# One-bank score units in an attention core, and re-ordered start and end of a state-space stage

## Time and profile before

| | us |
|---|---|
| median of 3 runs | 2258.87 |
| lowest and highest | 2258.38, 2261.21 |
| the profiled execution, its own time | 2256.16 |
| its span (first to last instruction) | 2253.9 |
| mean granted clock of TensorE | 0.987 of full |

### The profile page before, as it was taken

The page is one execution under the profiler, slowest core; times in us unless marked ns, Lnnn a source line. Parts: engine busy times, 40 slices in busy tenths (PEclk is TensorE's granted clock), DMA queues, the critical chain, the costliest instruction groups (busy, mean ns, idle before and its releaser), DMA issues. The chain is left out here.

```text
span 2253.9 us, 34737 instructions
## 1 busy us (share of the span) xinstructions
PE 2149.1 (95%) x12556; PEld 1748.4 (78%) x12556; DVE 1676.1 (74%) x2693; ACT 1434.7 (64%) x3086; POOL 1038.2 (46%) x759
## 2 busy tenths in 40 slices
PE   7889989999899999999999999999999999997999
PEld 7856677887688878878887887887887888785887
DVE  7667755133688898889889889889988988986221
ACT  4377734333877677677777767766877677673332
POOL 5466535443146344444435533634445443545442
PEclk9999999999999999999999999999999999998999
DMA  3000012331333233223322323223322322231332
GB/s 131 1 1 1 1 43 61 94 94 57 141 113 108 94 117 122 85 86 140 122 85 85 141 94 113 97 94 129 107 100 85 141 108 100 85 113 40 92 95 83
DMA packets 64151, 202.50 MB, mean 90 GB/s; under 512 B 7024, under 2 KB 8048, under 8 KB 55664
## 3 DMA queue, kind: packets, MB, share of 16 engines
q1 hardware_dynamic: 63984, 200.31, 25.9%
HBM read 197.39 MB, written 2.88 MB: 89 GB/s over the span
## 5 line engine op out<-in xcount | busy, mean ns | idle before, releaser
L529 POOL TENSOR_TENSOR wAl<-rawA,wAh 128x512 fp32r<-128x512 f32 x233 | 325.8, 1411 | 406.1 <-ACT wAh L670 405.4
L1599 PE MATMUL ps<-xTh,wAh 128*128 128x512 f32 x1512 | 427.3, 404 | 7.9 <-DVE oacc L1437 3.0
L1599 PE MATMUL ps<-xTl,wAh 128*128 128x512 f32 x1512 | 415.0, 396 | 0.0
L1599 PE MATMUL ps<-xTh,wAl 128*128 128x512 f32 x1512 | 413.9, 395 | 0.0
L1332 DVE SCALAR_TENSOR_TENSOR work<-ps,chp,work 128x510 f32<-128x510 f32 (+2 forms) x465 | 343.5, 744 | 51.6 <-ACT work L829 41.6
L1599 PEld LDWEIGHTS ps<-xTl,wAh 128*128 128x128 f32 x1512 | 284.9, 188 | 69.7
L1599 PEld LDWEIGHTS ps<-xTh,wAh 128*128 128x128 f32 x1512 | 276.6, 189 | 78.4 <-issue 17.5
L1599 PEld LDWEIGHTS ps<-xTh,wAl 128*128 128x128 f32 x1512 | 283.6, 188 | 69.3
L535 POOL TENSOR_TENSOR wBl<-rawB,wBh 128x512 fp32r<-128x512 f32 x108 | 142.2, 1330 | 386.1 <-ACT wBh L674 386.1
L866 ACT ACTIVATE eb<-eb,gc 128x128 f32<-128x128 f32 x1008 | 307.7, 391 | 18.0 <-DMA eb<-scr_decays 18.0
L579 POOL TENSOR_TENSOR sqt<-gt 128x512 f32<-128x512 f32 x112 | 154.4, 1379 | 120.6 <-DVE gt L1391 112.1
(11 more groups left out here) (202 smaller groups left out, 3958.5 us busy)
## 6 DMA issues: line engine op xcount, KB each, us to landing
eb<-scr_decays SPq DMA_DIRECT2D x63, 1536.0 KB, 6.4
rawA<-ma_in SPq DMA_DIRECT2D x144, 256.0 KB, 3.6
rawA<-fa_in SPq DMA_DIRECT2D x88, 256.0 KB, 2.6
rawB<-mb_in SPq DMA_DIRECT2D x64, 256.0 KB, 2.8
rawB<-fb_in SPq DMA_DIRECT2D x44, 256.0 KB, 2.6
x<-x_in SPq DMA_DIRECT2D x8, 256.0 KB, 6.2
x_out<-x SPq DMA_DIRECT2D x8, 256.0 KB, 2.7
wqraw<-wqkv_in SPq DMA_DIRECT2D x1, 1536.0 KB, 10.9
```

Of the source, the lines that this page charges most:

```text
L529: nc.gpsimd.tensor_tensor(wAl[:, slot, :], rawA[:, slot, :], wAh[:, slot, :].bitcast(F32), ALU.subtract).then_inc(A_lo, 1)
L1599: return nc.tensor.matmul(o, l, r, start=start, stop=end, **kw)
```

## The change

All parts are order and tiling; the result is the same function.

- Attention. A unit is at most one bank: a narrow unit as before, a wide one in two halves h of two heads by 256 keys each, so there are 24 of them for a batch. They rotate over banks 2 to 5, so TensorE waits for the exponentials of the fourth unit back. The mask matmul of a half has 256 columns. The maximum is negated in the reduction itself, the factor 1/4 is put into the copy of the keys, and the small second instruction is gone. Transposes to banks 6 and 7 are signalled separately. On TensorE the order inside a wide unit is scores h=0, (value products), transposes of bank 6, scores h=1, transposes of bank 7. The last tile's head transposes move behind the scores of unit 3; the fill of the second key block on GpSimd moves ahead of the last tile's split.
- Start of the state-space stage. The chunk-end sums are copied out first (`end_sums`) and TensorE waits for that copy alone. The rows for step 1 are loaded straight after the first rows, and their chunk starts come as plain sums, exponentiated in place by `second_exp`.
- End. The swiglu's first four weight tiles are loaded, and split on ScalarE and GpSimd, one step earlier; the last step's decays, `scale_x` and transposes move ahead; `y_products` come before the `last_out` of the step before; ScalarE squares the last step's y into xdt, and `last_squares` sums sq and xdt with twice the matmuls.

The phrase "rebuilt expert stages" in the name of the change has nothing in the diff: the experts' code is the same on both sides. The core of the diff:

```diff
...
+    UNITS = 24
+    def unit(n, h=0):
+        b, s = n // 16, n % 16
+        return UNITS * b + (s if s < 8 else 8 + 2 * (s - 8) + h)
+    def unit_heads(n, h):
+        return range(4) if n % 16 < 8 else range(2 * h, 2 * h + 2)
+    def second_halves(n):
+        return 8 * (n // 16) + max(0, n % 16 - 7)
...
+            else:
+                for u in range(4):
+                    load_A(a0 + u, fa_in[u // 2, u % 2])
             for h in range(2):
                 for f in range(NF):
                     for u in range(2):
-                        load_A(a0 + (h * NF + f) * 2 + u, fa_in[f, u])
+                        n = (h * NF + f) * 2 + u
+                        if first or n >= 4:
+                            load_A(a0 + n, fa_in[f, u])
...
         first_rows(1)
+        sp.dma_start(eb[:, 1, :, 0:NT, :], scr[2:4, 0:NT, :].partition_broadcast(P)).then_inc(m_rows[1], 16)
+        for h in range(2):
+            sp.dma_start(eb[:, 1, h, NT:NT + B, :],
+                         scr[2 + h, 1:NT:2, :].partition_broadcast(P)).then_inc(m_second, 16)
         mamba_B(2, 0)
...
         sp.wait_ge(m_scr, 48)
-        mamba_rows(1, 0)
...
+            if t == NT - 1:
+                pool.wait_ge(a_proj, NT)
+                nc.gpsimd.memset(kBD[1][:, :, :, :, :].bitcast(F32), 0.0).then_inc(pads, 1)
+            if AHEAD + 2 <= t + 3 < NT:
+                layer_rstd(1, t + 3)
             pool.wait_ge(a_qh, t + 1)
             nc.gpsimd.tensor_tensor(qk[:, t % 2, 0:NH, HD:2 * HD].bitcast(F32R), qs[:, t % 2, :, :],
                                     qk[:, t % 2, 0:NH, 0:HD], ALU.subtract).then_inc(a_ql, 1)
...
+            if 3 <= t < 7:
                 pool.wait_ge(a_ql, t + 1)
-                key_lo(0, t - 4)
-                pool.wait_ge(a_kl, t - 3)
-        pool.wait_ge(a_proj, NT)
-        nc.gpsimd.memset(kBD[1][:, :, :, :, :].bitcast(F32), 0.0).then_inc(pads, 1)
+                key_lo(0, t - 3)
+                pool.wait_ge(a_kl, t - 2)
...
                 lo_A(A0G + i, g, NA_G)
+            if last and v == TPG - 2:
+                for u in range(4):
+                    lo_A(A0F + u)
...
         def finish():
-            for u in range(4):
-                lo_A(A0F + u)
-            lo_B(B0F)
-            square(TPG - 1, NG - 1, 0)
             last_rstd(0)
-            square(TPG - 1, NG - 1, 1)
             for t in range(AHEAD):
                 layer_rstd(5, t)
             last_rstd(1)
...
+        def exps(n, h):
+            m = unit(n, h)
+            heads = unit_heads(n, h)
+            wide = S if n % 16 >= 8 else P
+            act.wait_ge(a_nm, m + 1)
+            for i, j in enumerate(heads):
+                last = nc.scalar.activation(
+                    probs(n)[:, 0:wide // P, j, :],
+                    ps[:, 2 + m % 4, i * wide:(i + 1) * wide].rearrange("p (c k) -> p c k", k=P), ACT.Exp,
+                    bias=nm[:, m % 4, i:i + 1], accum_out=sm[:, n % RS, j:j + 1])
+            last.then_inc(a_exp, 1)
...
-                nk = 1 + s // 8
-                bank = 2 + 2 * (n % 2)
-                act.wait_ge(a_nm, n + 1)
+                if n == 2:
+                    act.wait_ge(a_qkt, NT - 1)
+                elif n == 3:
+                    queries(NT - 1)
                 if n >= PS_SLOTS:
                     act.wait_ge(a_tr, n - PS_SLOTS + 1)
+                    act.wait_ge(a_tr2, second_halves(n - PS_SLOTS))
                 if n >= RS:
                     act.wait_ge(a_rc, n - RS + 1)
-                for j in range(4):
-                    nc.scalar.activation(probs(n)[:, 0:nk, j, :],
-                                         ps[:, bank:bank + nk, j * P:(j + 1) * P], ACT.Exp,
-                                         bias=nm[:, n % 2, j:j + 1], scale=HD ** -0.5,
-                                         accum_out=sm[:, n % RS, j:j + 1]).then_inc(a_exp, 1)
+                exps(n, 0)
+                if s >= 8:
+                    exps(n, 1)
...
+            ending = last and v == TPG - 2
+            if ending:
+                hi_A(A0F)
+                hi_A(A0F + 1)
...
+            if ending:
+                hi_A(A0F + 2)
+                hi_A(A0F + 3)
...
-            decay_exp(*vn, 0)
-            decay_exp(*vn, 1)
+            if first and v == 0:
+                second_exp()
+            if not ending:
+                decay_exp(*vn, 0)
+                decay_exp(*vn, 1)
...
         def finish():
-            for u in range(4):
-                hi_A(A0F + u)
+            for p in range(2):
+                y_hi(NG - 1, TPG - 1, p)
+                nc.scalar.activation(xdt[:, 4 * p:4 * p + 4, :].rearrange("p t q -> p (t q)"),
+                                     gt[:, (TPG - 1) % 2, 512 * p:512 * p + 512], ACT.Square).then_inc(m_lsq, 1)
...
+        def end_sums(p):
             act.wait_ge(m_end, p + 1)
             nc.scalar.activation(wdt[:, 2 * p:2 * p + 2, :],
-                                 ps[:, YBANK[p], 0:2 * P].rearrange("p (b h) -> p b h", b=2), ACT.Exp).then_inc(m_u, 1)
+                                 ps[:, YBANK[p], 0:2 * P].rearrange("p (b h) -> p b h", b=2),
+                                 ACT.Copy).then_inc(m_ends, 1)
+        def end_decays():
+            act.wait_ge(m_ends, 2)
+            nc.scalar.activation(wdt[:, :, :], wdt[:, :, :], ACT.Exp).then_inc(m_u, 1)
+        def second_exp():
+            act.wait_ge(m_second, 32)
+            e = eb[:, 1, :, NT:NT + B, :].rearrange("p h t q -> p h (t q)")
+            nc.scalar.activation(e, e, ACT.Exp)
...
-        conv_silu(0, 4)
         conv_silu(0, 1)
         conv_silu(0, 3)
         gate_silu(0, 6)
+        end_sums(0)
+        end_sums(1)
+        conv_silu(0, 4)
+        conv_silu(0, 5)
         token_sums(1)
+        gate_silu(0, 7)
         spans(0, 0, 0)
-        conv_silu(0, 5)
-        gate_silu(0, 7)
-        hi_A(A0G + 5)
-        end_decay(0)
-        end_decay(1)
+        end_decays()
         first_exp(0)
         spans(0, 0, 1)
         first_exp(1)
+        hi_A(A0G + 5)
...
+            def negated_max(n, h):
+                m = unit(n, h)
+                heads = len(unit_heads(n, h))
+                dve.wait_ge(a_s, m + 1)
+                nc.vector.tensor_reduce(nm[:, m % 4, 0:heads], ps[:, 2 + m % 4, :].rearrange("p (j k) -> p j k", j=heads),
+                                        op=ALU.max, axis=AX.X, negate=True).then_inc(a_nm, 1)
...
-                    nk = 1 + n % 16 // 8
-                    bank = 2 + 2 * (n % 2)
-                    dve.wait_ge(a_s, n + 1)
-                    link(nc.vector.tensor_reduce(
-                        mx[:, n % 2, :], ps[:, bank:bank + nk, :].rearrange("p c (j k) -> p j c k", j=4),
-                        op=ALU.max, axis=AX.XY))
-                    if n >= 2:
-                        dve.wait_ge(a_exp, 4 * (n - 1))
-                    nc.vector.tensor_scalar(nm[:, n % 2, :], mx[:, n % 2, :], -HD ** -0.5, None,
-                                            ALU.mult).then_inc(a_nm, 1)
...
+                    negated_max(n, 0)
...
+                if n < N and n % 16 >= 8:
+                    negated_max(n, 1)
+                if 0 <= n - 1 < N:
+                    n1 = n - 1
+                    dve.wait_ge(a_exp, unit(n1, 1 if n1 % 16 >= 8 else 0) + 1)
...
+                if n == 3:
+                    keys(NT - 1)
...
+            elif k == 1:
+                dve.wait_ge(m_second, 32)
+                dve.wait_ge(m_exp, 3)
...
+            ending = last and v == TPG - 2
+            if ending:
+                decay_off(v + 1, g, 0)
+                decay_off(v + 1, g, 1)
...
+            if ending:
+                decay(v + 1, g, 0)
+                decay(v + 1, g, 1)
+                scale_x(v + 1, g, 0)
+                scale_x(v + 1, g, 1)
...
+            def scores(n, h):
+                b, s = n // 16, n % 16
+                qc, tt, r = s // 8, s // 4 % 2, s % 4
+                m = unit(n, h)
+                if m >= 4:
+                    pe.wait_ge(a_exp, m - 3)
+                t = 2 * b + qc
+                q = (xTh, xTl)[tt][:, r, t * P:(t + 1) * P]
+                to = ps[:, 2 + m % 4, :]
+                if qc == 0:
+                    mm(to, identb[:, :], negb[:, :, :].rearrange("p j k -> p (j k)"), True, False)
+                    mm(to, q, kBD[b % 2][:, 0, tt, :, 0:P], False, False)
+                    last = mm(to, q, kBD[b % 2][:, 1, tt, :, 0:P], False, True)
+                else:
+                    hi, lo = (kBD[b % 2][:, z, tt, 2 * h:2 * h + 2, :].rearrange("p j k -> p (j k)") for z in range(2))
+                    mm(to, q, hi, True, False)
+                    mm(to.rearrange("p (j k) -> p j k", j=2)[:, :, P:S], identb[:, :], negb[:, 0:2, :], False, False)
+                    last = mm(to, q, lo, False, True)
+                last.then_inc(a_s, 1)
...
-            pe.wait_ge(a_qt, 2 * NT)
-            pe.wait_ge(a_kt, NT)
-            pe.wait_ge(a_v, NT)
```

(51 more changed lines are left out.)

186 lines of the change are left out of this document (82 added, 104 removed).

## The result

The changed kernel takes 2221.5 us (median of four runs, 2220.6 to 2223.9) against 2259.6 for the kernel before on the same chip: ratio 0.9834, 95% interval 0.9822 to 0.9845, so 38 us less. The forecast was 2221.0, with a range from 2207 to 2238. The profiled execution of the changed kernel is the slowest of its four: own time 2223.9, span 2222.1, against 2256.2 and 2253.9 before.

What follows compares the result with a forecast made beforehand. TensorE is fullest, but in attention the chain around four engines sets the pace. Terms -14 - 6.5 - 2 - 6.5 - 9 = -38 take the profiled 2256.16 to 2218.2; the median, 2.7 above, gives 2221 us, range 2207 to 2238.

Steps and rivals of the forecast that it cites:

- Attention, steady part: Attention batches: four rotating banks loosen the coupling of engines, a batch falls from 43.9 to 40 us, -14 in all.
- the sum over quarters: Attention batch: largest engine load over each four units, work sliding only within them; 9.3, 9.2, 9.4, 11.6, sum 39.5 us.
- Rival 1: Attention units stay in step, so only start and tail gain, and perhaps 1 a batch; total -27.5, 2231; chance 0.17.
- rival 2: Attention: TensorE becomes the bound, a batch takes 36 to 37.5; total -49, 2210; chance 0.12.
- Rival 4: Attention: second-half scores come late behind transposes of unit n - 4; slower, 2273 at 1.2 a unit; chance 0.04.
- Attention, start and tail: Attention's ends: first scores fill TensorE's wait for the last tile's split, -6.5; tail transposes come closer together, -2.
- Start of the state-space stage: First state-space steps: rows for step 1 issued early, so ScalarE runs on without waiting for them; -6.5.
- A wait of 7.0 goes: State-space start: ScalarE's stand of 7.01 us until the rows for step 1 land disappears through their early issue.
- Rival 3: State-space start: early rows collide with the first rows on the DMA engines, start gains nothing; 2227; chance 0.06.
- End: Last state-space step: TensorE's waits for squares and decays, 8.52 us together, go; -9 (-6 to -11).
- The 7.58: State-space end: TensorE's wait for squares behind GpSimd's tile splits, removed as splits and squares both leave that place.
- the 0.94: State-space end: TensorE's wait for the last step's decays, 0.94 us, removed by moving them ahead of skip and gate.

Runs made afterwards that it cites:

- tile_wait: Changed kernel, but scores wait again for every exponential of the tile before last, with banks, halves and signals as changed: 2232.5 us (0.9878).
- heads_first: Changed kernel, but the last tile's head transposes stand before the first attention scores again: 2229.3 us (0.9864).
- start alone: Kernel before with only the rebuilt start of the state-space stage: 2254.3 us (0.9979).
- end alone: Kernel before with only the rebuilt end of the state-space stage: 2251.1 us (0.9965).

## Why the prediction was right

**Attention, steady part.** Forecast 40 a batch, measured 40.78; -14, measured -12.6. The term that was off is the sum over quarters: it gave 9.3, 9.2, 9.4, 11.6; the quarters measured from maximum to maximum (184.07, 193.11, 204.31, 212.68, 224.85) are 9.0, 11.2, 8.4, 12.2. Units 4 to 7 take 2.0 more than forecast, and this quarter gained nothing: before it was 11.1 (209.65 to 220.74). The matmuls that open the scores of unit 4 and of unit 8 say where the 2.0 is:

```profile
192.23 0.38 PE L1678 MATMUL ps<-negb,identb 128*128 128x512 bf16 x1
...
202.60 0.48 PE L1678 MATMUL ps<-kBD,xTh 128*128 128x512 f32 x1
```

In these 10.4 us TensorE does what the forecast counted for the quarter, 9.2 from start to start; the other 1.2 are three hand-overs of 0.3 to 0.5 (ahead of the value products, and twice ahead of transposes that wait for VectorE's copy of bank 6), which the sum over quarters put at nothing. The last 0.8 is on VectorE, where a copy, a reciprocal and an update of x stand between the scores of unit 8 and its maximum. TensorE's busy time there (9.96 of the 10.71 us from 193.60 to 204.31) hides this, since it counts drains. That scores wait for exponentials, and that four banks take this away, was right: `tile_wait` shows it for 9.6 of the 14.9. The 32.65 of VectorE was not the bound; taking 3.2 away gave 0.95. Rival 1 (units stay in step) would have shown a batch at 43, rival 2 one below 37.5; neither did. Rival 4 would need the second half to be late behind its transposes: interleaving is 0.3 a batch better than putting both halves first. (Its price for being slower is the 24 of the other gains and 5 more, 29, not less 5.)

**Attention, start and tail.** -6.5 and -2, measured -6.8 and -2.3. The working left out one thing that helps: before, TensorE came out of its wait at half clock (below). The delay of the last split by the clearing was foreseen as about a microsecond, and `heads_first` puts it at 1.5 (6.55 from tile 6's transposes to tile 7's, 5.08 before).

**Start of the state-space stage.** -6.5, measured -7.3 up to step 1 and -6.4 from step 1's SiLUs on; the kernel with this part alone gives -4.6 (-6.8 to -2.7). "A wait of 7.0 goes" holds, and "of TensorE's work the 3.56 goes, but then it waits for those decays instead" too: with the wait put back, nothing changes. Two terms in it were off. Of the wait of 7.0 the early issue removes 5.5, the smaller transfer the rest. And ScalarE's own work between the first spans and step 1's did not grow by 0.5 but shrank by 1.1, of which 0.8 was spent on later first spans. Rival 3 did not happen, though the transfer was slower there: the 1.0 MB took 8.4 from issue to landing (560.69 to 569.11), not 6.7, but ScalarE wanted it only at 573.28.

**End.** -9, measured -9.0, but the parts of the sum were not right one by one. The 7.58 did not need both splits and squares to leave. The decays were priced at the 0.94 that stood in the row; the run puts 5.0 on their move, since the products that covered them were moved behind and the wait brings the low clock with it. That the sum came out is luck in its terms: it took 8.52 of waits away and next to nothing else. Between the last spans and the evacuation TensorE's idle time falls from 8.52 to 1.51, by 7.0, since a wait of 1.51 is new ahead of the y products. The other 2.0 is its busy time, 21.8 to 19.9, at a granted clock of 0.89 before and 1.00 now: the low clock behind the old wait went with the wait. The switch of tables went by the row: ScalarE loads at 1992.37 and the exponential starts 1.29 later. But the step has one load more, not two: three (1989.90, 1992.37, 1996.30) where two stood (2014.15, 2025.45), and the last of them also serves the swiglu, whose own load at 2060.94 is gone; both executions have 135 in all. The 2.8 more that the forecast estimated from the Trainium skill ("ScalarE: Activation LUTs", What ACT_TABLE_LOAD costs) would have left 6.2; the stretch shows 9.0.

**The total.** Forecast 2221.0, measured 2221.5. That is closer than the parts: the steady part was forecast 1.4 better than it came out, and the start and tail of attention and the start of the state-space stage (up to step 1) together 1.4 worse. The hit to 0.5 is luck; that each of the five stretches came within 1.4 is not, though two of them did so by terms that offset each other.

## What to carry to other kernels

A wait in the trace is the remainder of something covered. When an edit moves the cover too, price the whole chain and not the row: the 0.94 was 5.0 here, 2.8 of it waiting and 2.2 matmuls at the low clock level. Where a ring of engines works in strict order, one more level of rotation can be worth more than work taken off the engine next to it: four banks against two gave 1.5 a batch, 3.2 us less of VectorE 0.95. And an engine's long wait ahead of an instruction does not mean that the instruction may be late: look for who waits for its result.

To judge a part worth less than the scatter of executions, measure between two instructions around it in each trace; here these distances mostly repeated to 0.2. And end the stretch late enough: a first evacuation that came 0.7 earlier was worth nothing by the second.

## What the runs showed of the hardware

**The clock around a wait.** Before, TensorE does nothing from 108.75 to 112.5 and then works at a granted clock of 0.50, the 1.2 GHz level, for at least the next 5.5 us; ten transposes take 2.37. In the changed kernel scores fill that wait, the granted clock stays 1.00 (2.4 GHz), and the same ten take 1.28. Filling a wait with work paid twice. Windows of the kernel before, then of the changed one:

```profile
108.75:112.50 3.75, 0.00 (x0) 0.02 (x1) 1.89 (x7) 2.34 (x4) 1.28 (x2) 0.98 0.00 0
112.50:118.00 5.50, 4.32 (x15) 3.23 (x16) 0.88 (x2) 1.09 (x2) 4.76 (x2) 0.50 0.02 3
```

```profile
108.75:112.30 3.55, 1.75 (x7) 0.79 (x6) 2.52 (x6) 2.98 (x15) 3.47 (x3) 1.00 0.02 5
112.30:118.00 5.70, 4.50 (x27) 3.26 (x27) 3.80 (x9) 5.70 (x30) 4.01 (x4) 1.00 0.00 0
```

**Identical code, two speeds.** Up to the first head transposes the code is the same in all kernels, and yet these start between 70.4 and 73.0. From 40 to 80 us the granted clock was 0.96 in the changed kernel's trace above and 0.91 in that of before:

```profile
40.00:80.00 40.00, 35.45 (x211) 33.44 (x210) 29.96 (x101) 12.35 (x26) 23.53 (x20) 0.91 0.01 1
```

Likewise the stretch from attention's last update of x to the first swiglu's first SiLU took 56.6 to 57.5 in six of the fourteen traces and 58.6 to 59.1 in the other eight, with kernels whose code up to there is the same on both sides (before 56.7, start alone and end alone 59.1 both). The window 319.70 to 341.70 above, with a clock of 0.84, is that loss of 2.4; the same window of the kernel before, 340.00 to 362.00, has 1.00. The tail of the new end is a third such place: from the first to the last evacuation it is 16.9 in the four traces with the old end and 17.0 to 19.8 in the ten with the new (18.2 in the changed kernel, with a granted clock of 0.51 from 2019.49 to 2024.49). Up to the end of the execution the two groups take the same, 209.8 to 212.3 and 209.7 to 212.7. Why one execution has such a stretch at the low clock and another doesn't, no run here settles.
